# Twelve late rounds of a fused attention-and-experts kernel: scores in two halves, U as three fp32r passes, softmax by pairs of tiles, silus in another place

## The chip, the cores and the metric

The kernel runs on one core of a Trainium2 chip. The metric is device time in microseconds (us) of one execution; lower is better. Times are given as the median of the runs shown. TensorE (PE) has a clock that the chip grants at one of two levels, 1.2 or 2.4 GHz; the profile shows the granted one as a share of full speed.

## The reference, cut to what matters

Eight sequences of 1024 tokens with 256 features. Each token is normalised; then attention runs over the four heads of one token (not over tokens), and the rows are laid out anew afterwards; a mixture of eight experts with top-2 gates gives the factor of its output.

```python
xn = layernorm(x)
q = (xn @ Wq + bq).reshape(b, s, h, d)           # h = 4, d = 256; k and v in the same way
qr, qi, kr, ki = q * cos, q * sin, k * cos, k * sin
scores = (einsum('bshd,bsgd->bshg', qr, kr) + einsum('bshd,bsgd->bshg', qi, ki)) / sqrt(d)
out = einsum('bshg,bsgd->bshd', softmax(scores), v)
out = swapaxes(out, 1, 2).reshape(b, s, h * d) @ Wo + bo
y = xn + sum over the top 2 experts e of gate_e * (relu(xn @ wg[e]) * (xn @ wp[e])) @ wo[e]
result = x + out * silu(y)
```

## The kernel before, in words

**Tiling.** The 8192 tokens are worked through in 16 rounds (q = 0 to 15, NQ = 16) of 512 tokens, four tiles of 128 each (n = 4q to 4q+3). Rounds 0 to 3 (QE = 4) run first, then the experts (135 tiles of 128 gathered tokens, each with its `up`, `ht` and `down`), then the twelve late rounds 4 to 15. Semaphores order everything; each engine follows its own written-out list, and nothing is moved by a scheduler.

**One late round on TensorE** (`segment` of the tensor block). Chunks c = 0 to 15 are projections: `L1082`, six fp32r matmuls of 512 columns each (two halves of the features times the three products of high and low parts, WH and WL of the weights, XH and XL of the tokens). Even-numbered and odd-numbered chunks hold the two halves of a head's features; c below 8 is q, the rest is k. ScalarE (`L819`, times cosine) and then VectorE (`L1598`, times sine) write the chunk rotated into QT. Chunks 16 to 23 are U, the tokens times M = Wv Wo folded per head, 512 columns each: `L1093`, two fp32 matmuls whose operands are XTJ (the sum of XH and XL in another order, made by GpSimd at `L578`) and M_s in SBUF. ScalarE copies each U chunk to UN (`L826`), SyncE writes it to `u_d` (`L325`) and loads it back in another layout as US (`L399`). Between the U chunks stand the mixes of the round before (`mix`, `L1050`: attention weights AT times US) and the transposes `xt` of the round after. Then come `scores` of four tiles, 32 fp32 matmuls of 64 columns each (`L1029`), on which VectorE does `soft_a`, ScalarE the Exp (`L840`), VectorE `soft_b`; `spread` builds AT for a tile in the next round.

**PSUM.** There are eight banks. A projection or U chunk may take its bank when ScalarE and VectorE are through with the chunk that had it before (`ring`). Projections of the late rounds take five banks in turn.

**The output of a round.** GpSimd's list for iteration q is `xtj(q)`, `total(q - 1)` (16 multiplies and adds of 128x256 on expert outputs that were loaded: `L663`, `L667`, `L670`), in rounds 5, 7, 9, 11 (`host`) also `total` of one of the early rounds, and `finish(q - 1)` (`L678`, `L679`). `total(q - 1)` feeds a Silu on ScalarE (`L806`; `silu(q - 1)`), placed after chunk 18 of round q, and that feeds `finish`. The Silu of an early round (`L802`) stands among the Exps behind the scores of a host round. SyncE's list at the end of round q, behind the last write of U, is: three loads of US, `reload_e` (`L443`, waits for the early Silu) or `store_e` (`L451`) in rounds 5 to 12, `store_c(q - 1)` (`L410`, waits for `finish(q - 1)`), `load_c(q)`: expert outputs and tokens (`L422` to `L424`) and, once the store has landed (same buffers), the x rows (`L428`). `total(q)` waits for all of `load_c(q)`.

In round 15 the mixes of its own tiles follow at the end, with a last `store_last`.

## Time and profile before

| | us |
|---|---|
| median of 3 runs | 1589.56 (1588.63 to 1591.09) |
| the profiled execution | 1596.37 |
| its span, first to last instruction | 1594.6 |
| late rounds: first projection of round 4 to the end of the span | 1009.4 to 1594.6 |

The profiled execution has 1.8 us around its span and lies 6.8 us above the median. TensorE is busy 96% of the span, VectorE 61%, GpSimd 50%, ScalarE 46%. In the rows, a fp32 matmul shows as two records, a matmul's duration overlaps the next one's, so that pace is read from starts; SPq rows are issues of DMAs by SyncE. Times in the timelines count from the start of the span.

### The profile page before, as it was taken

To read this page: it belongs to the slowest core of one execution; us is meant where nothing else is said; L and a number is where in the kernel's file an instruction comes from. 1 tells how busy PE (TensorE), PEld (TensorE's weight loads), DVE (VectorE), ACT (ScalarE), POOL (GpSimd) and SP (SyncE) were. 2 spreads that over 40 slices of the span, in tenths; PEclk is the share of its full clock that TensorE was granted. 3 is DMA by queue.
4 is the path that set the end of the run, shared out by engine and by line. 5 is a ranking of instruction groups with operands and counts; after the bars stand their busy time and mean duration, and the time that the engine had idled before them with its cause. 6 is when DMAs were issued, how large, how long until landed. Compare 5 with 4: busy or idle time off the path is not lost.

```text
span 1594.6 us, 32793 instructions
## 1 busy us (share of the span) xinstructions
PE 1533.0 (96%) x11408; PEld 1168.2 (73%) x11408; DVE 976.4 (61%) x1880; ACT 729.6 (46%) x1205; POOL 794.2 (50%) x945
## 2 busy tenths in 40 slices
PE   5999699989999999999999999999999999999997
PEld 2546565658888888888888888776666776666774
DVE  7567899953333333333333333577889788888777
ACT  4766334413333333333333333546456565555552
POOL 4637588913344434443344333253584564853456
PEclk9999899989999999999999999999999999999998
DMA  9989842266133232223211231255555666455464
GB/s 326 395 316 331 299 175 72 75 206 209 56 132 96 96 113 76 88 102 112 78 54 57 71 145 44 91 165 176 179 181 180 201 197 226 149 164 168 148 205 146
DMA packets 175351, 251.23 MB, mean 158 GB/s; under 512 B 15336, under 2 KB 122656, under 8 KB 175072
## 3 DMA queue, kind: packets, MB, share of 16 engines
q1 hardware_dynamic: 160576, 211.48, 38.8%
q0 software_dynamic: 12960, 35.41, 6.7%
q8 instruction: 104, 1.70, 0.4%
q10 hardware_dynamic: 1664, 2.26, 0.4%
q14 instruction: 47, 0.39, 0.1%
HBM read 149.58 MB, written 99.50 MB: 156 GB/s over the span
## 4 chain that ended last, share of the span: by engine, by line
PE 90%; DVE 6%; DMA 1%; ACT 1%; issue 1%; SPq 1%; ACTq 0%; DVEq 0%
PE ps L1147 24%; PE ps L1082 21%; PE ps L1093 13%; PE ps L1166 12%; PE ps L1029 7%; PE ps L1156 4%; PE ps L1050 2%; PE ps L1129 2%; PE ps L998 2%; PE ps L926 1%; PE ps L982 1%; PE ps L916 1%; DVE UN L1232 1%; DMA WR<-w_d 1%; DVE OH L1555 1%
## 5 line engine op out<-in xcount | busy, mean ns | idle before, releaser
L1147 PE MATMUL ps<-WR,FR 128*128 x1620 | 407.6, 401 | 2.3 <-DMA WR<-w_d 2.3
L1147 PEld LDWEIGHTS ps<-WR,FR 128*128 128x128 f32 x1620 | 295.8, 189 | 59.9 <-issue 2.5
L651 POOL DMA_INDIRECT y_d<-AUX x135 | 133.3, 987 | 353.0 <-ACT AUX L870 353.0
L1658 DVE TENSOR_TENSOR AUX<-AUX,ps 128x512 f32<-128x512 f32 x135 | 93.0, 689 | 341.2 <-ACT AUX L858 341.2
L819 ACT ACTIVATE WM<-ps,bcs,trig 128x512 f32<-128x512 f32 x256 | 253.1, 1016 | 90.7 <-PE ps L1082 83.4
L1598 DVE TENSOR_SCALAR WM<-ps,vec,trig 128x512 f32<-128x512 f32 x256 | 244.4, 993 | 62.7 <-ACT WM L819 62.0
L1093 PE MATMUL ps<-WM,XTJ 128*128 128x512 f32 x512 | 237.1, 600 | 0.0
L858 ACT ACTIVATE AUX<-ps 128x512 f32<-128x512 f32 x135 | 80.9, 599 | 317.5 <-PE ps L1147 282.8
L1082 PE MATMUL ps<-XH,WH 128*128 128x512 f32 x512 | 205.2, 401 | 4.8 <-issue 3.8
L1166 PE MATMUL ps<-WR,ABR 128*128 x1080 | 209.4, 292 | 0.0
L1082 PE MATMUL ps<-XL,WH 128*128 128x512 f32 x512 | 200.2, 391 | 0.0
L1082 PE MATMUL ps<-XH,WL 128*128 128x512 f32 x512 | 200.0, 391 | 0.0
L646 POOL DMA_INDIRECT AUX<-xn_d,AUX x135 | 131.6, 975 | 75.3 <-issue 40.0
L1166 PEld LDWEIGHTS ps<-WR,ABR 128*128 128x128 f32 x1080 | 165.5, 190 | 0.0
L1093 PEld LDWEIGHTS ps<-WM,XTJ 128*128 128x128 f32 x512 | 91.6, 190 | 96.6 <-issue 93.8
L663 POOL TENSOR_TENSOR AUX<-AUX,GP 128x256 f32<-128x256 f32 x128 | 81.2, 669 | 150.1 <-DMA AUX<-in_L_attn_x_dram 145.4
L1166 PE MATMUL ps<-WR,FR 128*128 x540 | 152.0, 281 | 0.0
L1029 PE MATMUL ps<-WM 128*64 128x64 f32 x4096 | 131.4, 228 | 18.0 <-DVE TM L1486 16.7
L1029 PEld LDWEIGHTS ps<-WM 128*64 128x64 f32 x4096 | 127.4, 143 | 26.9 <-DVE TM L1486 17.1
L826 ACT ACTIVATE UN<-ps 128x512 f32<-128x512 f32 x128 | 76.2, 595 | 139.4 <-PE ps L1093 135.9
L1082 PEld LDWEIGHTS ps<-XH,WH 128*128 128x128 f32 x512 | 96.6, 189 | 25.7 <-issue 5.0
L1082 PEld LDWEIGHTS ps<-XH,WL 128*128 128x128 f32 x512 | 96.5, 189 | 20.6
(238 smaller groups left out, 2202.9 us busy)
## 6 DMA issues: line engine op xcount, KB each, us to landing
US<-u_d SPq DMA_DIRECT2D x63, 512.0 KB, 4.8
u_d<-UN SPq DMA_DIRECT2D x120, 256.0 KB, 2.0
WR<-w_d SPq DMA_DIRECT2D x96, 256.0 KB
AUX<-y_d SPq DMA_DIRECT2D x32, 512.0 KB, 5.5
WM<-in_L_attn_x_dram SPq DMA_DIRECT2D x16, 512.0 KB, 9.6
xn_d<-WM SPq DMA_DIRECT2D x32, 256.0 KB, 7.4
w_d<-USR SPq DMA_DIRECT2D x16, 512.0 KB, 4.2
AUX<-xn_d SPq DMA_DIRECT2D x16, 512.0 KB, 6.1
```

Source lines behind the costliest of these rows:

```text
L646: e.indirect_dma_start(XG[m % 4], None, xn_d, bass.IndirectOffsetOnAxis(gidx[:, m:m + 1], 0)).then_inc(s_g[m % 4], 16)
L651: e.indirect_dma_start(y_d, bass.IndirectOffsetOnAxis(toks[:, n:n + 1], 0), YS[n % 4], None).then_inc(s_y[n % 4], 16)
L663: ins = e.tensor_tensor(y[:, i, :], y[:, i, :], GP[:, i, k, q, None].broadcast_to([128, D]), ALU.mult)
L819: e.activation(rotated(2 * x, i), b, ACT.Identity, bias=bcs[:, x, 0, i:i + 1], scale=trig[:, 0, i:i + 1]).then_inc(s_ca, 1)
L858: e.activation(GR[:, :], mG[m % 2][:, :], ACT.Relu).then_inc(s_gr, 1)
L1029: mm = e.matmul(pS[n % 2][row:row + 64, 64 * c:64 * c + 64].rearrange("p (g t) -> p g t", g=H), QT[:, x, h, col:col + 64], QT[:, 2 + x, h, ...
L1082: mm = e.matmul(b[:, :], w[:, k, 128 * c:128 * c + 128], xx[:, k, :], start=(k == 0 and w is WH and xx is XH), stop=(k == 1 and w is WL))
L1093: mm = e.matmul(b[:, :], XTJ[:, k, a // 2, :], M_s[:, k, 512 * a:512 * a + 512], start=(k == 0), stop=(k == 1))
L1147: mm = e.matmul(b[:, :], x, WR[:, bass.ds(off[m] + (2048 * z + 1024 * a + 512 * k), 512)], start=(k == 0 and x is xh and z == 0), stop=(k ...
L1166: mm = e.matmul(mY[m % 2][:, 0:256], x, WR[:, bass.ds(off[m] + (4096 + 1024 * z + 256 * c), 256)], start=(c == 0 and x is hh and z == 0), ...
L1598: e.tensor_scalar(rotated(2 * x + 1, i), ps[bank(24 * q + c)][:, :], bqk[:, x, i:i + 1], trig[:, 1, i:i + 1], ALU.add, ALU.mult).then_inc( ...
L1658: e.tensor_tensor(HS[:, m % 2, :], GR[:, :], mP[m % 2][:, :], ALU.mult).then_inc(s_h, 1)
```

## The change

Only the late rounds (q from 4 on) and the expert stage are changed.

- **U in three fp32r passes.** In the expert stage ScalarE's queue loads M from `m_d` in 16 pieces, VectorE splits each into a high and a low part (`split_m`), ScalarE's queue stores both in `mhl_d`. Behind the experts' weights SyncE loads the low part to ML and the high part to MH (in place of M_s). A U chunk is then six fp32r matmuls: XHJ by MH, XHJ by ML, XLJ by MH, for both halves of the features. GpSimd's `xj` makes XHJ and XLJ with eight copies of 256 columns (before: `xtj`, four additions).
- **Order of a round.** Rounds 4 to 14: the eight even chunks, U 16 to 19, first half of all scores (`half_scores(q, 0)`, step 24), the eight odd chunks, U 20 to 23, second half. Round 15: even chunks, all of U, first half, odd chunks, second half, then its mixes. QT becomes QH, half the size, which the odd chunks fill again. The number of score matmuls is the same; all four tiles gather in two banks.
- **Banks.** Even chunks take 0,1,6,7,2,0,1,2 (round 4: 0,1,4,5,2,0,1,2), odd ones 1,2,6,7,0,1,2,0.
- **Mixes** stand behind chunk 19, step 24, chunk 21 and chunk 23 (before: 18, 20, 22, 23); transposes behind 20 and 22 (before: 17, 20).
- **VectorE** does `soft_a2`, `soft_b2`, `spread2` for two tiles in one instruction each; one Exp serves two tiles.
- **Silus on ScalarE.** `silu(q - 1)` stands at step 24: behind the copy of U 19 and ahead of the eight odd rotations. `silu(host[q])` stands behind U 20. In round 15, `silu(15)` stands behind chunk 5 of the odd ones, and the x rows of round 15 are loaded late (`load_x`).

The diff, cut to its core:

```diff
+        def order(q):
+            if q < QE:
+                return tuple(range(24))
+            if q < NQ - 1:
+                return P0 + (16, 17, 18, 19) + P1 + (20, 21, 22, 23)
+            return P0 + tuple(range(16, 24)) + P1
+        BANKS = {c: (0, 1, 6, 7, 2, 0, 1, 2)[i] for i, c in enumerate(P0)}
+        BANKS.update({c: (1, 2, 6, 7, 0, 1, 2, 0)[i] for i, c in enumerate(P1)})
...
+            def xj(q):
+                e.wait_ge(s_xtd, 2 * q + 2)
+                e.wait_ge(s_ch, 24 * q)
+                for k in range(2):
+                    for v, w in ((XHJ, XH), (XLJ, XL)):
+                        for j in range(2):
+                            ins = e.tensor_copy(v[:, k, 2 * j:2 * j + 2, :],
+                                                w[:, k, :].rearrange("p (r j) -> p j r", j=4)[:, 2 * j:2 * j + 2, :])
+                    ins.then_inc(s_xtj, 1)
...
-                    for c in range(24):
-                        e.wait_ge(s_ch, 24 * q + c + 1)
-                        b = ps[bank(24 * q + c)][:, :]
+                    for c in steps(q):
+                        if c == 24:
+                            if q > QE:
+                                silu(q - 1)
+                            continue
+                        e.wait_ge(s_ch, at(q, c))
...
-                        if q > QE and c == 18:
-                            silu(q - 1)
-                        if q == NQ - 1 and c == 23:
+                        if q == NQ - 1 and c == 5:
                             silu(q)
+                        if q in host and c == 20:
+                            silu(host[q])
...
+            def split_m(i):
+                e.wait_ge(s_mr, 16 * (i + 1))
+                ch(e.tensor_copy(UNR[:, 1, :], UN[:, 0, :]))
+                e.tensor_tensor(UNR[:, 2, :], UN[:, 0, :], UNR[:, 1, :].bitcast(F32), ALU.subtract).then_inc(s_msp, 1)
...
                             for k in range(2):
-                                mm = e.matmul(b[:, :], XTJ[:, k, a // 2, :], M_s[:, k, 512 * a:512 * a + 512],
-                                              start=(k == 0), stop=(k == 1))
+                                for xx, w in ((XHJ, MH), (XHJ, ML), (XLJ, MH)):
+                                    mm = e.matmul(b[:, :], xx[:, k, j, :], w[:, k, cols],
+                                                  start=(k == 0 and xx is XHJ and w is MH), stop=(k == 1 and xx is XLJ))
```

ScalarE's list for one late round of the kernel before, from the end of one round's projections on (L819 rotation, L826 copy of U, L755 copy of the transposed tokens, L806 Silu of the round before with its table load, L840 Exp):

```order
L819 ACTIVATE WM<-ps,bcs,trig 128x512 x16
L826 ACTIVATE UN<-ps 128x512 x2
L755 ACTIVATE XH<-ps 128x512
L826 ACTIVATE UN<-ps 128x512
L806 ACT_TABLE_LOAD
L806 ACTIVATE AUX<-AUX 128x1024
L826 ACTIVATE UN<-ps 128x512 x2
L755 ACTIVATE XH<-ps 128x512
L826 ACTIVATE UN<-ps 128x512 x3
```

The same stretch of the changed kernel (L926 rotation, L935 copy of U, L855 tokens, L906 Silu, L949 Exp):

```order
L926 ACTIVATE WM<-ps,bcs,trig 128x512 x8
L935 ACTIVATE UN<-ps 128x512 x4
L906 ACT_TABLE_LOAD
L906 ACTIVATE AUX<-AUX 128x1024
L926 ACTIVATE WM<-ps,bcs,trig 128x512 x8
L935 ACTIVATE UN<-ps 128x512
L855 ACTIVATE XH<-ps 128x512
L935 ACTIVATE UN<-ps 128x512 x2
L855 ACTIVATE XH<-ps 128x512
L935 ACTIVATE UN<-ps 128x512
```

The Silu stood behind all sixteen rotations and three copies of U; now eight rotations stand behind it.

ScalarE's last round of the changed kernel, where both Silus of the end stand:

```order
L926 ACTIVATE WM<-ps,bcs,trig 128x512 x8
L935 ACTIVATE UN<-ps 128x512 x8
L906 ACT_TABLE_LOAD
L906 ACTIVATE AUX<-AUX 128x1024
L926 ACTIVATE WM<-ps,bcs,trig 128x512 x3
L906 ACTIVATE AUX<-AUX 128x1024
L926 ACTIVATE WM<-ps,bcs,trig 128x512 x5
L949 ACT_TABLE_LOAD
L949 ACTIVATE AC<-AC 128x32 x2
```

In the kernel before, the last Silu stood behind the last copy of U, with no rotation after it; now five rotations and the second half of the scores follow.

TensorE's list at the end of a late round, before (L1093 U, L1050 mix, L1029 scores, all four tiles):

```order
L1093 MATMUL ps<-WM,XTJ 128x512 x4
L1050 MATMUL ps<-US,AT 32x256 x4
L1093 MATMUL ps<-WM,XTJ 128x512 x2
L1050 MATMUL ps<-US,AT 32x256 x4
L1029 MATMUL ps<-WM 64x64 x128
```

And in the changed kernel (L1260 U, L1114 transposes, L1204 mix, L1181 half of the scores):

```order
L1114 MATMUL ps<-ident,XB 128x128 x4
L1260 MATMUL ps<-WR,XHJ 128x512 x2
L1260 MATMUL ps<-WR,ABR 128x512
L1260 MATMUL ps<-WR,XHJ 128x512 x2
L1260 MATMUL ps<-WR,ABR 128x512
L1204 MATMUL ps<-US,AT 32x256 x4
L1181 MATMUL ps<-WM 64x64 x64
```

One U chunk is six matmuls where it was two, and 64 instead of 128 score matmuls lie between the last write of U and the next round's first projection.

## Rows read from the trace of the kernel before

**Rows 1.** TensorE's timeline (start, duration, engine, line, operation): projections.
```profile
1009.40 0.47 PE L1082 MATMUL ps<-XH,WH 128*128 128x512 f32 x1
...
1056.42 0.50 PE L1082 MATMUL ps<-XH,WH 128*128 128x512 f32 x1
...
1246.32 0.50 PE L1082 MATMUL ps<-XH,WH 128*128 128x512 f32 x1
...
1251.67 0.39 PE L1082 MATMUL ps<-XH,WL 128*128 128x512 f32 x1
1251.90 0.39 PE L1082 MATMUL ps<-XH,WH 128*128 128x512 f32 x1
```

**Rows 2.** TensorE's timeline: scores of round 4; first U and last mix of round 8.
```profile
1048.81 7.68 PE L1029 MATMUL ps<-WM 128*64 128x64 f32 x256
...
1220.18 3.59 PE L1093 MATMUL ps<-WM,XTJ 128*128 128x512 f32 x8
...
1237.18 0.64 PE L1050 MATMUL ps<-US,AT 128*32 128x256 f32 x8
```

**Rows 3.** ScalarE's timeline: rotations; Silu and last U copy of round 8.
```profile
1106.68 10.13 ACT L819 ACTIVATE WM<-ps,bcs,trig 128x512 f32<-128x512 f32 x9
...
1219.02 0.78 ACT L819 ACTIVATE WM<-ps,bcs,trig 128x512 f32<-128x512 f32 x1 [0.58 <-PE ps L1082]
...
1226.58 1.28 ACT L806 ACT_TABLE_LOAD   x1
1227.87 1.06 ACT L806 ACTIVATE AUX<-AUX 128x1024 f32<-128x1024 f32 x1
...
1237.29 0.60 ACT L826 ACTIVATE UN<-ps 128x512 f32<-128x512 f32 x1 [1.89 <-PE ps L1093]
```

**Rows 4.** SyncE's timeline: issues at the end of rounds 5, 8, 14.
```profile
1088.93 7.40 SPq L325 DMA_DIRECT2D u_d<-UN  x4
...
1237.91 0.32 SPq L325 DMA_DIRECT2D u_d<-UN  x1
...
1241.59 4.13 SPq L451 DMA_DIRECT2D out_dram<-AUX  x4
1245.76 3.56 SPq L410 DMA_DIRECT2D out_dram<-AUX  x4
...
1251.32 2.73 SPq L428 DMA_DIRECT2D AUX<-in_L_attn_x_dram  x4
...
1516.15 7.39 SPq L325 DMA_DIRECT2D u_d<-UN  x4
```

**Rows 5.** GpSimd's timeline: totals of rounds 7 and 8, tokens for U.
```profile
1214.10 5.38 POOL L663 TENSOR_TENSOR AUX<-AUX,GP 128x256 f32<-128x256 f32 x8 [16.07 <-DMA AUX<-in_L_attn_x_dram]
...
1222.42 3.82 POOL L670 TENSOR_TENSOR AUX<-AUX 128x256 f32<-128x256 f32 x4
...
1239.89 4.53 POOL L578 TENSOR_TENSOR XTJ<-XH,XL 128x256 f32<-128x256 f32 x4
1259.32 4.61 POOL L663 TENSOR_TENSOR AUX<-AUX,GP 128x256 f32<-128x256 f32 x8 [14.90 <-DMA AUX<-in_L_attn_x_dram]
...
1266.91 2.80 POOL L670 TENSOR_TENSOR AUX<-AUX 128x256 f32<-128x256 f32 x4
```

**Rows 6.** VectorE's timeline: a strided and a plain rotation.
```profile
1208.07 1.19 DVE L1598 TENSOR_SCALAR WM<-ps,vec,trig 128x512 f32<-128x512 f32 x1 [0.19 <-ACT WM L819]
...
1219.83 0.81 DVE L1598 TENSOR_SCALAR WM<-ps,vec,trig 128x512 f32<-128x512 f32 x1 [0.55 <-ACT WM L819]
```

**Rows 7.** TensorE's timeline in round 15: first projection, two mixes.
```profile
1530.68 0.50 PE L1082 MATMUL ps<-XH,WH 128*128 128x512 f32 x1
...
1578.10 0.66 PE L1050 MATMUL ps<-US,AT 128*32 128x256 f32 x8 [2.81 <-DVE AT L1513]
...
1586.48 1.10 PE L1050 MATMUL ps<-US,AT 128*32 128x256 f32 x8 [2.71 <-DVE AUX L1540]
```

**Rows 8.** One window of 1 us (granted clock third from the end).
```profile
1580.00:1581.00 1.00, 1.00 (x25) 1.00 (x24) 0.90 (x4) 0.00 (x0) 0.19 (x1) 0.50 0.99 340
```

More of the change, by code:

```diff
@@ L428, in load_c, with load_x @@
                     e.dma_start(xx[h:128:4], rows(xf, q)[h]).then_inc(sl, 16)
+            def load_x():
+                e.wait_ge(s_ch, at(NQ - 1, 17))
+                for h in range(H):
+                    e.dma_start(cs(NQ - 1)[3][h:128:4], rows(xf, NQ - 1)[h]).then_inc(s_xe, 16)
             def load_e(k):
@@ L840, in segment @@
                         e.activation(SE[:, n % 2, :], SS[:, n % 2, :], ACT.Exp, scale=1.0 / 16).then_inc(s_exp, 1)
-                        if i == 1 and q in host:
-                            silu(host[q])
             e.wait_ge(s_trig, 1)
@@ L1033, in scores, with half_scores @@
                 mm.then_inc(s_s, 1)
+            def half_scores(q, h):
+                e.wait_ge(s_ca, at(q, 14 + h))
+                e.wait_ge(s_cd, rotated_by[q, 14 + h])
+                if h == 0:
+                    e.wait_ge(s_sm1, 4 * q)
+                for i in range(4):
+                    for c in range(4):
+                        for x in range(2):
+                            for a in range(2):
+                                row = 64 * a
+                                col = 128 * (4 * i + c) + row
+                                to = 256 * (i % 2) + 64 * c
+                                mm = e.matmul(pS[i // 2][row:row + 64, to:to + 64].rearrange("p (g t) -> p g t", g=H),
+                                              QH[:, x, col:col + 64],
+                                              QH[:, 2 + x, :].rearrange("p (g t) -> p g t", g=H)[:, :, col // 4:col // 4 + 16],
+                                              start=(h == x == c == i % 2 == 0),
+                                              stop=(h == x == i % 2 == 1 and c == 3))
+                    if h == 1:
+                        mm.then_inc(s_s, 1)
             def mix(n):
@@ L1076, in segment @@
                     e.wait_ge(s_xtd, 2 * q + 2)
-                    for c in range(24):
-                        b = ring(24 * q + c)
+                    for c in steps(q):
+                        if c == 24:
+                            half_scores(q, 0)
+                            if c in mixes(q):
+                                mix(4 * q - 4 + mixes(q)[c])
+                            continue
+                        b = ring(q, c)
                         if c < 16:
@@ L1109, in segment @@
                         scores(4 * q + i)
[L1110 to L1111 removed]
                         place(lists.get((q, 24 + i), ()))
                 if q1 == NQ:
[L1114 to L1115 removed]
+                    e.wait_ge(s_ca, at(NQ - 1, 15))
+                    e.wait_ge(s_cd, rotated_by[NQ - 1, 15])
+                    for i in range(4):
+                        mix(4 * NQ - 4 + i)
             e.wait_ge(s_wsp, 4)
@@ L1613, in segment @@
                             early(host[q - 1])
-                        if q + 1 < q1 and c in (17, 20):
-                            xt(q + 1, c // 20)
+                        if q + 1 < q1 and c in turns(q):
+                            xt(q + 1, turns(q)[c])
+                    n = 4 * q
+                    if q >= QE:
+                        soft_a2(n)
+                        soft_a2(n + 2)
+                        soft_b2(n)
+                        if q < NQ - 1:
+                            soft_b2(n + 2)
+                            continue
+                        spread2(n)
+                        soft_b2(n + 2)
+                        spread2(n + 2)
+                        for i in range(4):
+                            mixed(n + i)
+                        continue
                     if q == QE - 1:
@@ L1629, in segment @@
                     soft_b(4 * q + 3)
-                if q1 == NQ:
-                    spread(4 * NQ - 1)
-                    for i in range(1, 4):
-                        mixed(4 * NQ - 4 + i)
             segment(0, QE)
```

247 lines of the change are left out of this document (192 added, 55 removed).

## The prediction

> **What bounds the kernel now.** I read the page first: TensorE is busy 96% of the span and the chain that ended last is 90% TensorE. Then TensorE's timeline, round by round. An undisturbed late round lasts 1056.42 - 1009.40 = 47.0 us from first projection to first projection [rows 1], and no gap of note is in it, so TensorE bounds the late rounds. A cut of its work is therefore worth its full size, until something else sets the round. To find what that is I followed, in the timelines of ScalarE, SyncE and GpSimd, the one loop that runs from round to round beside TensorE: last U copy, SyncE's queue, load, `total`, Silu. In the kernel before it has hardly any slack: the total of round 7 ends at 1222.42 + 3.82 = 1226.24, and the Silu that waits for it starts at 1227.87, behind a table load from 1226.58 on [rows 3, 5]. The reader should see there that the data come late, and that only the place of the Silu, 27 us into the round, hides it. The change moves this place.
>
> **TensorE's saving.** U: eight records of a fp32 matmul take from 1220.18 on 3.59 us, of which 0.16 overlaps what follows, so 0.43 each [rows 2]; 32 records per round make 13.7 us. The three passes are 8 x 6 = 48 fp32r matmuls of 512 columns. Their nearest row is the projection, same size and type: 1251.90 - 1251.67 = 0.23 [rows 1], exactly 1.36 per chunk of six, so 10.9 us. Saved: 2.8 us, and with one mix and two transposes breaking up U no more often than before I take 3.0, a round of 44.0 us. Scores keep their 128 matmuls, 7.7 us [rows 2], 3.85 per half; mixes (0.57 each, 1237.75 - 1237.18) and transposes are moved only. Bounds for a U chunk: 1.36 and the 1.72 of now, since nothing else of that kind is in the trace; I take the first. Twelve rounds would gain 36 us if nothing else decided.
>
> **Expert stage.** Added there: 16 loads and 16 stores on ScalarE's queue, 32 VectorE instructions (about 1 us per seven tiles), 12.6 MB of transfers and 4 MB more of loads. From 560 to 1030 us TensorE is busy without a break while VectorE is busy under 40%, ScalarE likewise, and the DMA engines a quarter. A tile takes 4.8 us and each product of VectorE is wanted most of a tile later. Cost zero; were that cover gone it would be 16 us at most. The M parts are in SBUF long before round 4, as the experts' last 17 tiles lie behind the last expert load.
>
> **xj.** Eight GpSimd copies replace four strided additions of 4.53 us together, 1.1 each [rows 5]. A copy reads one operand: between 0.4 and 1.1 us each, 3 to 9 us. It starts with the last mixes of a round, some 4 us ahead of the next one's start, and U now wants it 10.9 us into the round instead of 21.8. It fits even at 9 us. Zero.
>
> **Where the stall goes: the Silu.** `silu(q-1)` now stands behind U 19 [the order of ScalarE], that is 10.9 (even chunks) + 5.4 (four U) + 1 = 17.5 us into the round; before, 27. Behind it are the eight odd rotations. While ScalarE waits there, TensorE goes on with the first half of the scores, a mix and the five odd chunks whose banks are free (1, 2, 6, 7, 0), and then stands still at chunk 11, which wants bank 1 from chunk 1. I work out the loop from the last U write of one round to that of the next, as if it closed:
>
> 1. Last U write to total done. Round 8: the write is issued by 1238.23, then come the loads of US, `store_e`, `store_c`, the loads of `load_c` (last x issue ends at 1254.05), landing, total from 1259.32 to 1269.71 [rows 4, 5]: 31.5 us. The same reading in rounds 6, 10, 12, 13, 14 gives 29.7, 30.5, 29.4, 29.3, 30.2. In host rounds SyncE also waits 4 to 6 us for the early Silu; without this wait, which the change removes, and with an unslowed total they give 28.4 to 30.1. Mean of all ten: 29.7.
> 2. A total that runs beside VectorE's `spread` and `biased` is slower: 1214.10 to 1226.24 is 12.1 us against 10.4 for 1259.32 to 1269.71 [rows 5]. In the changed order it runs 16 to 27 us into the round, beside three `biased` and one `spread2`. Between 0 and 1.7; I take 1.4.
> 3. Silu: 1.06, table load already done while waiting, hop 0.1 [rows 3]: 1.2.
> 4. From the Silu's end to the next last U write. ScalarE's strided rotations take 1.17 each (10.13 less one of 0.78, over 8) [rows 3], VectorE follows 0.19 later with 1.18 [rows 6]. So chunk 1 leaves bank 1 at 2.6 and TensorE does chunk 11 until 4.0 and 13 until 5.4; chunk 15 wants bank 0 from chunk 9, free at 6.9 (four strided rotations and a plain one, VectorE's at 0.81), and ends at 8.3. Then four U (5.4), two transposes (0.9), one mix (0.6): 15.3; copy and issue 1.0 as at 1237.29 to 1238.23 [rows 3, 4]: 16.3.
>
> Sum 29.7 + 1.4 + 1.2 + 16.3 = **48.6 us per round**, above the 44.0 of TensorE's own work: the loop does close, and TensorE loses 4.6 us in each round. In the kernel before, the nine rounds from the last U write of round 5 (1096.33) to that of round 14 (1523.54) [rows 4] took 427.2, or 47.5 each.
>
> **The clock.** TensorE stands still for about 3 us at chunk 11. After a gap of 2.81 us the trace shows the granted clock at 0.50, that is 1.2 GHz, in a window that begins 2 us behind the gap [rows 7, 8]. If that happens here, chunks 11 and 13 take about 1.7 us more, but chunk 15 waits for VectorE until 6.9 anyway, so 0.2 is left. Zero in the sum.
>
> **The total.** Round 4 has no Silu and gains 3.0. Round 5's total is ready early (loaded long before), so its end of U comes 2.2 earlier: TensorE's saving twice, 6.0, less the half of the scores that now stands ahead of the last U. Rounds 6 to 14: 9 x 48.6 = 437.4, against 427.2: +10.2. Round 15, from the last U write of round 14: before 1594.6 - 1523.5 = 71.1. After: 3.3 to the round's start (half a set of scores), then 27.9 for even chunks, U, half the scores and four mixes; odd chunks run, but `silu(15)` behind chunk 5 wants a second total, which GpSimd ends at 27.8 + 10.4 = 38.2; Silu until 39.4, chunks 7 and 9 rotated until 42.6, chunk 15 until 44.1, rotated by 46.0, second half of the scores until 49.9. Then softmax and spread of pairs, about 4.8 (VectorE's pieces of two tiles), four mixes at the low clock, 1.96 each (1586.48 to the next at 1588.4 by its records) [rows 7], and 3.5 for the last product and store: 66, and 1 for scores at the low clock after the long wait. 70.3, so -0.8. Sum: -2.2 + 10.2 - 0.8 = **+7.2 us**. The profiled span would be 1601.8; the median, 6.8 below the profiled execution before, goes from 1589.56 to **1596.8 us**. What 0.1 us in the loop means here: 0.9 us in the end.
>
> **A rule of the skill.** The rows show a total slowed by 1.7 us by about four us of VectorE work in SBUF. The Trainium skill (SBUF — State Buffer, "SBUF: two separate sides") says that a VectorE instruction with two SBUF inputs and a GpSimd one that reads SBUF exclude each other for the whole instruction. By it, an estimate, the three `biased` (1.2 each) and two products would hold the total up by their full 4 us instead of 1.4; that result is the fourth rival below.
>
> **Rivals.**
> 1. *The saving arrives* (not slower): something makes the total come in time, and the round is TensorE's 44.0. What decides is whether loop parts 1 to 3 end within 28 us of the last write. Eleven rounds at -3.0, the last one as above without its 5 us stall: about -35, 1555 us. Against it: the shortest of ten readings is 28.4, before any slowing and the Silu. Chance 0.09.
> 2. *A shorter loop*: parts 1 and 2 at their low ends (28.6 and 0), the last part 0.5 less because VectorE's rotations overlap by 0.1 each: 46.2 to 47.4. 9 x -1.2 to -2.4 off the forecast: 1575 to 1586 us. For it: SyncE no longer waits for the early Silus, so transfers may spread better. Chance 0.17.
> 3. *The low clock counts*: it falls at chunk 11 and again at chunk 15, and the four U of the last part run at 1.2 GHz too: 1.7 us more in each of nine rounds, +15: 1612 us. For it: a gap of 2.8 us has been enough in the trace. Against it: chunks 11 to 15 are nearly unbroken work. Chance 0.10.
> 4. *GpSimd and VectorE exclude each other*: a total held up by 4 us instead of 1.4: 9 x 2.6 = 23, but in the rows both slow a little, and the 12.1 us total had as much beside it. 1620 us. Chance 0.04.
> 5. *The change does not do what it says*: U's passes cost as much as fp32, or xj comes late. Behind the stall both have some cover of their own, so the time stays near 1600. Chance 0.02, counted with the forecast.
>
> **How the numbers follow.** The forecast (loop closes at 47.5 to 49.9) has 0.60; of it 0.45 are slower by over 0.2%, 0.13 within, 0.02 faster. A difference of 0.2%, 3.2 us, is about what a measurement of this kernel can tell from none. Rivals 3 and 4 are slower (0.14), rival 1 faster (0.09), rival 2 faster with 0.15 and within with 0.02. Together: faster 0.26, same 0.15, slower 0.59. The range: loop bounds 47.5 to 49.9 give 1587 to 1609; rival 2 and rival 3 up to 1614 are taken in, so 1574 to 1614; rival 1, rival 4 and the tails are left out, about 0.18.
>
> **What the profile after would show.** Right: ScalarE idle ahead of the first odd rotation for 8 to 10 us in rounds 6 to 14, put down to GpSimd's last addition or to the Silu; TensorE's projections of odd chunks waiting for VectorE's rotation, two gaps of 2 to 3 and 1 to 2 us per round; first projections 48 to 49 us apart, but 44 from round 4 to round 5; U passes 0.23 apart; DMA landing 15 us into a round. Wrong: rounds of 44 us, a total that starts before 10 us into the round, or a gap that ends with GpSimd's xj ahead of U 16.

## The result, and the profile after

| | before | after |
|---|---|---|
| median, us | 1590.12 (4 runs beside it) | **1625.3** (4 runs, 1618.91 to 1630.5) |
| ratio to before | | **1.0205**, 95% interval 1.0178 to 1.0232 |
| span of the profiled execution, us | 1594.6 | 1628.7 |
| mean granted clock | 0.986 | 0.979 |
| round 4, first projection to first projection, us | 47.0 | 44.3 |
| rounds 5 to 14, the same, mean, us | 47.4 | 50.7 |
| round 15, first projection to the end, us | 63.9 | 68.8 |

The kernel became 2% slower. The forecast had the sign and the place right and was 28 us short: 1596.8 us forecast, and the time lies above the range of 1574 to 1614. Of the 35 us that the change costs it had seen 7.

TensorE's timeline of the kernel after (start, duration, engine, line, operation), at the first projection of rounds 4, 5 and 6. These rows answer to [rows 1]:

```profile
1008.47 0.47 PE L1241 MATMUL ps<-XH,WH 128*128 128x512 f32 x1
...
1052.74 0.50 PE L1241 MATMUL ps<-XH,WH 128*128 128x512 f32 x1
...
1104.79 0.50 PE L1241 MATMUL ps<-XH,WH 128*128 128x512 f32 x1
```

The reader sees the promised saving once: 1052.74 - 1008.47 = 44.3 us for round 4, against 47.0. The next one takes 52.1. One round in detail, number 8. TensorE (answers to [rows 2]):

```profile
1223.00 0.39 PE L1260 MATMUL ps<-WR,ABR 128*128 128x512 f32 x1
...
1223.68 0.39 PE L1260 MATMUL ps<-WR,ABR 128*128 128x512 f32 x1
...
1224.57 3.95 PE L1181 MATMUL ps<-WM 128*64 128x64 f32 x128
...
1235.75 0.39 PE L1241 MATMUL ps<-XH,WL 128*128 128x512 f32 x1
1239.14 0.59 PE L1241 MATMUL ps<-XH,WH 128*128 128x512 f32 x1 [3.00 <-DVE WM L1810]
1239.53 0.63 PE L1241 MATMUL ps<-XL,WH 128*128 128x512 f32 x1
```

Three U passes take 1223.68 - 1223.00 = 0.68, so 0.23 each, and a half of the scores 3.95: both as forecast. Then TensorE stands still for 3.00 us ahead of chunk 11, and goes on at 0.39 to 0.43 a matmul, from start to start, where it was 0.23. ScalarE in the same round (answers to [rows 3]); the number in brackets is the idle time ahead of an instruction, and what ended it:

```profile
1225.21 0.60 ACT L935 ACTIVATE UN<-ps 128x512 f32<-128x512 f32 x1 [1.87 <-DMA u_d<-UN]
1225.83 1.28 ACT L906 ACT_TABLE_LOAD   x1
1235.56 1.06 ACT L906 ACTIVATE AUX<-AUX 128x1024 f32<-128x1024 f32 x1 [8.45 <-POOL AUX L769]
```

GpSimd's total, which the Silu waits for (answers to [rows 5]):

```profile
1223.16 5.26 POOL L762 TENSOR_TENSOR AUX<-AUX,GP 128x256 f32<-128x256 f32 x8 [14.43 <-DMA AUX<-in_L_attn_x_dram]
1228.51 3.00 POOL L766 TENSOR_TENSOR AUX<-AUX 128x256 f32<-128x256 f32 x4
1231.59 3.94 POOL L769 TENSOR_TENSOR AUX<-AUX 128x256 f32<-128x256 f32 x4
```

And SyncE's U writes that close the loop, the last of round 7 and of round 8 (answers to [rows 4]):

```profile
1199.06 3.30 SPq L395 DMA_DIRECT2D u_d<-UN  x3
...
1247.13 6.13 SPq L395 DMA_DIRECT2D u_d<-UN  x4
```

The loop can be read off: last write ends at 1202.36, total from 1223.16 to 1235.53, Silu from 1235.56 to 1236.62, next last write ends at 1253.26. That is 20.8 + 12.4 + 1.1 + 16.6 = 50.9 us. The waits in sum, TensorE's and ScalarE's from 1009 to 1629 us (engine, line, what was waited for: us, times, longest):

```profile
PE ps L1241 <- DVE WM L1810: 32.2, 21, 3.5
...
ACT AUX L906 <- POOL AUX L769: 67.1, 11, 9.4
...
ACT UN L935 <- DMA u_d<-UN: 26.0, 6, 8.2
```

### The profile page after: what moved, and what is told of

Read it like the earlier page. It is cut to its first block, busy times and chain, and to the rows that moved or that the text cites. A ratio compares the mean times of both kernels' runs of the same rounds, so it can differ in the third digit from the quotient of the medians.

```text
span 1628.7 us, 33088 instructions
## 1 busy us (share of the span) xinstructions
PE 1519.5 (93%) x11600; PEld 1211.5 (74%) x11600; DVE 933.3 (57%) x1640; ACT 702.6 (43%) x1173; POOL 813.7 (50%) x993
## 4 chain that ended last, share of the span: by engine, by line
PE 65%; POOL 9%; DMA 8%; DVE 7%; SPq 6%; ACT 3%; issue 2%; ACTq 0%; DVEq 0%; POOLq 0%
PE ps L1318 23%; PE ps L1337 12%; PE ps L1241 10%; POOL AUX L762 4%; PE ps L1260 4%; PE ps L1327 4%; POOL AUX L769 3%; DMA out_dram<-AUX 3%; DMA AUX<-in_L_attn_x_dram 3%; POOL AUX L766 2%; PE ps L1256 2%; PE ps L1300 2%; PE ps L1130 2%; DVE WM L1810 2%; PE ps L1058 1%
## 5 line engine op out<-in xcount | busy, mean ns | idle before, releaser
L750 POOL DMA_INDIRECT y_d<-AUX x135 | 138.9, 1029 | 347.1 <-ACT AUX L983 347.1
L1810 DVE TENSOR_SCALAR WM<-ps,vec,trig 128x512 f32<-128x512 f32 x256 | 233.9, 993 | 83.6 <-ACT WM L926 83.3
L926 ACT ACTIVATE WM<-ps,bcs,trig 128x512 f32<-128x512 f32 x256 | 237.9, 1011 | 92.2 <-PE ps L1241 89.4
L1241 PE MATMUL ps<-XH,WH 128*128 128x512 f32 x512 | 213.3, 417 | 40.0 <-DVE WM L1810 33.1
L1241 PE MATMUL ps<-XL,WH 128*128 128x512 f32 x512 | 205.2, 401 | 0.0
L762 POOL TENSOR_TENSOR AUX<-AUX,GP 128x256 f32<-128x256 f32 x128 | 90.4, 740 | 136.2 <-DMA AUX<-in_L_attn_x_dram 133.0
L935 ACT ACTIVATE UN<-ps 128x512 f32<-128x512 f32 x128 | 76.5, 598 | 145.3 <-PE ps L1260 79.8
L1260 PE MATMUL ps<-WR,XHJ 128*128 128x512 f32 x384 | 123.7, 403 | 7.8 <-issue 4.9
L1241 PEld LDWEIGHTS ps<-XL,WH 128*128 128x128 f32 x512 | 99.4, 194 | 18.3 <-issue 0.2
L691 POOL TENSOR_SCALAR OH<-AUX 128x128 bf16<-128x128 f32 x96 | 95.1, 1002 | 23.9 <-DVE AUX L1604 15.6
L1181 PEld LDWEIGHTS ps<-WM 128*64 128x64 f32 x3072 | 93.6, 140 | 16.3 <-issue 12.9
```

The costliest lines, as they stand in the source:

```text
L691: e.tensor_scalar(rank1h[:, j % 16, :], ior_f, slot_p[:, k, n:n + 1], mark[:, k, n:n + 1], ALU.is_equal, ALU.mult).then_inc(s_oa, 1)
L750: e.indirect_dma_start(y_d, bass.IndirectOffsetOnAxis(toks[:, n:n + 1], 0), YS[n % 4], None).then_inc(s_y[n % 4], 16)
L762: ins = e.tensor_tensor(y[:, i, :], y[:, i, :], GP[:, i, k, q, None].broadcast_to([128, D]), ALU.mult)
L926: e.activation(rotated(q, 2 * x, i), b, ACT.Identity, bias=bcs[:, x, 0, i:i + 1], scale=trig[:, 0, i:i + 1]).then_inc(s_ca, 1)
L1181: mm = e.matmul(pS[i // 2][row:row + 64, to:to + 64].rearrange("p (g t) -> p g t", g=H), QH[:, x, col:col + 64], QH[:, 2 + x, :].rearrange ...
L1241: mm = e.matmul(b[:, :], w[:, k, 128 * c:128 * c + 128], xx[:, k, :], start=(k == 0 and w is WH and xx is XH), stop=(k == 1 and w is WL))
```

## The experiments

All experiment kernels share one small edit of the expert stage (how two engines read a count). The first run shows that it costs nothing, and the others are read against it. "A round" in the table is the mean of rounds 5 to 14, from first projection to first projection.

| kernel | median, us | ratio to before (95%) | a round, us |
|---|---|---|---|
| control: after, with this edit | 1624.13 | 1.0218 (1.0192 to 1.0245) | 50.1 |
| Silus later | 1595.83 | 1.0028 (1.0008 to 1.0048) | 46.8 |
| total without its products | 1591.68 | 1.0007 (0.9988 to 1.0026) | 46.5 |
| loads for the total first | 1609.05 | 1.0123 (1.0085 to 1.0161) | 48.9 |
| before, with an early Silu | 1675.83 | 1.0547 (1.0525 to 1.0569) | 55.6 |
| total of quarter 4 behind the softmax | 1618.69 | 1.0186 (1.017 to 1.0203) | 49.5 |
| no bias added beside the total | 1596.56 | 1.0036 (1.002 to 1.0052) | 48.0 |
| early quarter's loads later, alone | 1628.1 | 1.0235 (1.0217 to 1.0252) | 50.4 |
| Silus later and three repairs | 1575.43 | 0.9913 (0.9897 to 0.993) | 45.9 |
| the same, early quarter's loads later | **1567.6** | **0.9863** (0.9844 to 0.9883) | 45.3 |
| the same, loads for the total first | 1576.76 | 0.993 (0.991 to 0.9949) | 45.7 |

### Control

```diff
-                e.reg_load(wreg[m % 2], ewl[0:1, m:m + 1])
-                e.wait_ge(s_wl, e.snap(wreg[m % 2], min_val=192, max_val=192 * E))
+                e.wait_ge(s_wl, e.value_load(ewl[0:1, m:m + 1], min_val=192, max_val=192 * E))
```

> The changed kernel with only the two register reads of the expert stage written in another form (TensorE's count of expert loads, SyncE's count of tiles): nothing of the late rounds is touched. Every theory expects 1625 us within 4, the same 50.6 us per late round and the same expert stage. It is the base from which the other runs are read.

Measured 1624.13 us. The late rounds show the same waits: ScalarE 61.8 us for GpSimd's last addition, nine times.

### Undo the place of the Silu

```diff
                         if c == 24:
-                            if q > QE:
+                            if q == NQ - 1:
                                 silu(q - 1)
...
-                        if q in host and c == 20:
+                        if QE < q < NQ - 1 and c == 20:
+                            silu(q - 1)
+                        if q in host and c == 23:
                             silu(host[q])
```

> Only the place of the Silu on ScalarE changes, in rounds 5 to 14: silu(q-1) from behind U 19 to behind U 20's copy (after the odd rotations), the Silu of an early round's quarter from behind U 20 to behind U 23. Theory (the loop last U write, load, total, Silu, rotations, last U write sets the round only because eight rotations stand behind the Silu): total is done 33 us after the last write, that is about 30 us into the round, and U 20 is copied at about 37, so nothing waits; rounds fall from 50.6 to 44.0 to 45.0, nine of them by 50 to 59 us, time 1566 to 1578 us. Rival 1 (the halves of the scores, the softmax by pairs and the banks cost the 6.6 us per round): under 5 us of change. Rival 2 (the later Silu makes finish, the store and the next load later, and the loop closes again at about 47): 1590 to 1600 us.

Measured 1595.83: 28 us less than the control, not 50. The mechanism is confirmed and the size missed. ScalarE no longer waits for a total in rounds 5 to 14: each Silu of rounds 6 to 14 starts 8 to 11 us behind the end of its total. ScalarE's list of waits from 1053 to 1560 us has:

```profile
ACT WM L923 <- PE ps L1240: 79.7, 72, 6.3
...
ACT UN L932 <- DMA u_d<-UN: 43.9, 11, 9.4
```

The list has no line for the Silu any more. TensorE's own list from 1053 to 1525 us shows what remains, single gaps of 1.1 to 3.2 us and one small one per round (only behind the one of 1.91 us did the clock fall):

```profile
PE ps L1259 <- ACT WM L923: 5.2, 4, 1.6
PE ps L1180 <- issue: 4.5, 2, 2.6
PE ps L1240 <- DVE WM L1807: 3.9, 2, 3.2
```

Rival 2 names the time (1590 to 1600) but not the cause: the loop has slack here, since the Silu waits for nothing. What lies between 44.3 and 46.8 us per round is taken up below, with the repairs.

### Shorten the loop without touching the Silu

```diff
+                if q < QE:
                     for i in range(4):
                         for k, y in enumerate((y1, y2)):
                             ins = e.tensor_tensor(y[:, i, :], y[:, i, :], GP[:, i, k, q, None]...
```

> GpSimd's eight multiplications with the gates are left out of the total of quarters 4 to 15 (that part of the computation is missing); the Silu keeps its place. Theory (the loop decides): each loop is shorter by the 4.6 to 5.3 us of these eight, so rounds of 45.3 to 46.3 and 9 x 4.6 to 5.3 = 41 to 48 us less; round 5, where VectorE's subtraction of 5.19 us lies beside just these multiplications, gains another 4 to 5: 1572 to 1580 us. Rival (the total is not what decides): within 10 us of the control.

Measured 1591.68: 32 us less than the control, where 44 to 52 were expected (1572 to 1580 us). ScalarE's wait for the total falls from 61.8 to 16.8 us. Two edits that have nothing in common but the loop each take some 30 us away, so the loop set the round. The late Silus, with slack in the loop, show a second floor at 46.8 us, 2.5 above TensorE's 44.3. The 46.5 here is near it, but is not the same thing: in six of nine rounds the Silu still starts 0.03 us behind the total's end, and this profile is of the fastest execution (1580.7 us, 11 below the median).

### Shorten the loop on SyncE

```diff
-                        store_c(q - 1)
                         load_c(q)
...
                 e.dma_start(xn, blk(xn_d, q)).then_inc(sl, 16)
...
+                    store_c(q - 1)
                     e.wait_ge(s_o, 64 * (q - QE))
                 for h in range(H):
-                    e.dma_start(xx[h:128:4], rows(xf, q)[h]).then_inc(sl, 16)
+                    e.dma_start(xx[h:128:4], rows(xf, q)[h]).then_inc(s_cx, 16)
...
-                    e.wait_ge(*((s_cl, 112 * (q - QE + 1)) if q < NQ - 1 else (s_c15, 48)))
+                    e.wait_ge(*((s_cl, 48 * (q - QE + 1)) if q < NQ - 1 else (s_c15, 48)))
```

> SyncE issues the three loads that the total reads ahead of the four stores of the quarter before, and the total waits for these three alone, no longer for the four loads of x as well (which the later sum waits for). The Silu keeps its place. Theory (the loop decides, and its first part is SyncE's queue): the loads are issued 2.6 to 5.3 us earlier and the x loads (3 us) are no longer waited for, so the total starts 5 to 8 us earlier, 12 to 15 us behind the last write; rounds fall to 44 to 46, time 1570 to 1590 us. Rival (the loads are late for the transfers' own sake, or the total comes beside more VectorE work and gets slower): under 15 us of gain.

Measured 1609.05: 15 us less, on the edge of the rival. The total starts 14 to 18 us behind the last write, 3.3 earlier on average than in the control. In rounds 6, 8, 10, 12, 13 and 14 that shortens the loop, by 1.7 to 4 us. In rounds 7, 9 and 11, with an early quarter, it gets 1.4 to 2.8 us longer, as another wait takes the place of the old one. ScalarE and SyncE there:

```profile
1276.71 0.60 ACT L935 ACTIVATE UN<-ps 128x512 f32<-128x512 f32 x1 [12.81 <-DMA u_d<-UN]
...
1278.62 1.06 ACT L906 ACTIVATE AUX<-AUX 128x1024 f32<-128x1024 f32 x1
```

```profile
1262.93 2.62 SPq L503 DMA_DIRECT2D AUX<-in_L_attn_x_dram  x4
...
1268.72 0.51 SPq L517 DMA_DIRECT2D AUX<-xn_d  x1
```

The first U write stands on SyncE's queue behind the x loads, which wait for the stores, and behind the early quarter's loads. ScalarE waits 12.81 us for its U buffer and comes to the Silu 3.1 us after the total is done. I had counted what the edit takes off the loop, not what it puts ahead of the U writes.

### Only the place, in the kernel before

```diff
-                        if q > QE and c == 18:
+                        if q > QE and c == 9:
                             silu(q - 1)
```

> The kernel before, with one edit: in the late rounds silu(q-1) stands on ScalarE behind chunk 9 (14 us into the round) and no longer behind U 18 (27 us in). Nothing of the scores, of U or of the softmax is touched. Theory (the place of the Silu closes the loop whatever the forms are): total is done 30 us behind the last write, Silu 1.1, then rotations of chunks 10 to 15 and eight U of 1.8 and the write, about 20: a round of 50 to 52 against 47.4, so 25 to 40 us more, 1615 to 1630 us, with ScalarE waiting 8 to 12 us for GpSimd in each round. Rival (the new forms cost the time, the place alone does little): under 8 us more.

Measured 1675.83: 87 us more than the kernel before (1589.1 beside it), the direction of the theory and more than twice its size (25 to 40). ScalarE at a Silu, and SyncE at the last writes of two rounds:

```profile
1241.31 1.06 ACT L803 ACTIVATE AUX<-AUX 128x1024 f32<-128x1024 f32 x1 [11.52 <-POOL AUX L667]
```

```profile
1257.52 7.39 SPq L325 DMA_DIRECT2D u_d<-UN  x4
...
1311.62 7.40 SPq L325 DMA_DIRECT2D u_d<-UN  x4
```

The last writes end at 1206.63, 1264.91 and 1319.02. The second step, 54.1 us, is 29.9 (write to total done) + 1.1 + 23.1 (Silu to next last write): I had put the last part at 20. The first, 58.3, has 34.6 in its first part, because in these rounds SyncE also waits for the early quarter's Silu, which stood late in the kernel before. So the same formula gives these rounds too. It also shows what the change did beside moving the Silu: behind it stand 16 us in the kernel after, against 23 here, with four U chunks already done.

### Round 5: GpSimd keeps VectorE out

```diff
+                if q == QE + 1:
+                    e.wait_ge(s_sa2, 4 * QE + 4)
                 if QE < q < NQ:
                     total(q - 1)
```

> The changed kernel with one wait more: in round 5 GpSimd begins the total of quarter 4 only when VectorE has ended the softmax of round 4. Theory (a GpSimd multiplication in a row keeps VectorE's short subtraction out for 5 us, and this holds up the first rotation of round 5): the subtraction takes 0.3 to 0.7 us, the first rotation starts 5 us earlier, TensorE's gap of 3.17 us at 7.5 us into round 5 goes, with 1 to 2 us of low clock, and the time falls by 4 to 6 us: 1618 to 1621. Rival (the subtraction is slow for another reason): no change, 1624.

Round 5 of the kernel after has a row that no one expected. VectorE, then GpSimd:

```profile
1052.51 0.19 DVE L1702 TENSOR_REDUCE AC<-AC 128x8 f32<-128x32 f32 x1
1052.80 5.19 DVE L1703 TENSOR_TENSOR AC<-AC 128x32 f32<-128x32 f32 x1
```

```profile
1053.32 4.63 POOL L762 TENSOR_TENSOR AUX<-AUX,GP 128x256 f32<-128x256 f32 x8
1058.02 2.81 POOL L766 TENSOR_TENSOR AUX<-AUX 128x256 f32<-128x256 f32 x4
```

A subtraction of 32 columns takes 5.19 us and ends with the last of GpSimd's eight multiplications. The second pair's softmax, both Exp and ScalarE's first rotation stand behind it, and TensorE waits 3.17 us at chunk 11. With the wait added the same subtraction reads:

```profile
1050.74 0.60 DVE L1700 TENSOR_TENSOR AC<-AC 128x32 f32<-128x32 f32 x1
```

TensorE's gap in round 5 is gone and the time is 5.4 us less than the control's, as expected. The edit moves the total away from the softmax and changes nothing else there.

### What the total costs beside VectorE

```diff
                 u = US[:, n % 3, :, :]
+                if n >= 16:
+                    u = US[:, n % 3, 0:1, 0:8]
+                    e.tensor_tensor(u, u, BR[:, None, 0:8], ALU.add).then_inc(s_ub, 1)
+                    return
```

> The changed kernel with its Silu where it stands; VectorE's addition of the bias row to U (128x1024, 1.2 to 2.5 us, once per tile) is cut to eight columns from quarter 4's tiles on, so most of the bias is missing there. Theory (beside VectorE's additions the total is slowed from 10.4 to 13.1 us, and each us of it is a us of the loop): total 10.4 to 11.4 us, rounds shorter by 1.7 to 2.7, nine of them 15 to 24: 1600 to 1609 us. Rival (the slower total is not VectorE's doing, or the loop has slack there): totals stay at 13 and the time within 4 us of 1624.

Measured 1596.56: 27.6 us less than the control, more than the 15 to 24 expected. GpSimd's total in round 8 of this kernel:

```profile
1214.79 4.61 POOL L759 TENSOR_TENSOR AUX<-AUX,GP 128x256 f32<-128x256 f32 x8 [16.32 <-DMA AUX<-in_L_attn_x_dram]
1219.49 2.78 POOL L763 TENSOR_TENSOR AUX<-AUX 128x256 f32<-128x256 f32 x4
1222.34 3.05 POOL L766 TENSOR_TENSOR AUX<-AUX 128x256 f32<-128x256 f32 x4
```

10.6 us. The nine totals of rounds 6 to 14 take 10.6 to 11.0 in this kernel, where those of the kernel after take 11.8 to 13.9. The nine rounds 6 to 14 shrink from 50.2 in the control to 47.9 each, 21 us: 2.1 of the 2.4 per round is the shorter total (12.9 to 10.7), and 0.4 lies behind the Silu, where the clock stays at full speed in all nine rounds of this kernel. Another 4.5 us is in round 15, where a total of 14.3 us comes down to 10.7. VectorE's part that was left out is 1.2 us of work per tile and is hardly ever late itself (TensorE waits 0.7 us for it in the whole kernel after): it costs time through GpSimd.

### The early quarter's loads, and the repairs

> The changed kernel, only with the three loads of the early quarter behind the fourth U write in rounds 5, 7, 9 and 11; every Silu keeps its early place. Theory (the loop through the Silu decides, what is gained ahead of it is waited out at it): ScalarE's wait for the U buffers goes, its wait for the total grows by as much, TensorE's gaps put down to issue shrink; 0 to 6 us less, 1618 to 1624. Rival (SyncE's queue in these four rounds was the cost, as the last run suggests with its 8 us): 8 to 12 us less, 1612 to 1616.

```diff
-                    if q in host:
-                        load_e(host[q])
...
                         write_u(e, q, c)
+                        if q in host and c == 3:
+                            load_e(host[q])
```

Measured 1628.1, 4 us more than the control. ScalarE's waits from 1053 to 1560 us:

```profile
ACT AUX L903 <- POOL AUX L766: 77.3, 9, 9.3
ACT UN L932 <- DMA u_d<-UN: 12.7, 7, 2.8
```

In the control these are 61.8 and 31.7. What ScalarE no longer waits for its buffers it waits for the total: the loop takes back all that is gained ahead of it. TensorE's gaps within the scores shrink too, from 1.67 and 2.58 us in rounds 9 and 11 of the control to 0.30 and nothing above 0.3, and the time does not. The rival (8 to 12 us less) falls. The theory's mechanism holds, its number does not: 0 to 6 us less were expected, and why it is 4 more is open.

The repairs on top of the later Silus, beside the wait of round 5 shown above:

```diff
-                        if q - 1 in host and c == 8:
+                        if q - 1 in host and c == 22:
                             early(host[q - 1])
...
-                        if q == NQ - 1 and c == 5:
+                        if q == NQ - 1 and c == 15:
                             silu(q)
```

> The later Silus of the run above (1595.8 us), with three more edits: the wait of round 5 as in the run beside it; the host quarter's two VectorE sums (2.4 us) from behind chunk 8 to behind U 22, out of the way of the even rotations; silu(15) from behind chunk 5 to behind chunk 15. Theory (what is left over TensorE's 44.3 per round are small stalls, each followed by a stretch at half clock): round 5 gains 4 to 5; rounds 6, 8, 10 and 12 lose their gap of 1.1 to 1.6 us ahead of U 16 and gain 1.5 to 2.5 each, 8 together; round 15 loses its gap of 3.9 us ahead of chunk 7 and gains 3 to 4: 1578 to 1581 us, 12 faster than the kernel before. Rival (another stall takes their place, or the loop closes again): 1590 or more.

Measured 1575.43, a little better than expected. TensorE's gaps of 1.1 to 1.6 us ahead of U 16 in rounds 6, 8, 10 and 12 are gone, and so are those of 3.2 us in round 5 and 3.9 us in round 15. The three edits were made together; what each is worth was not measured here, only the wait of round 5 by itself above. With the early quarter's loads moved as well:

> As the run beside it, and in rounds 5, 7, 9 and 11 the three loads of the early quarter (1.5 MB) stand on SyncE behind the fourth U write and no longer ahead of the first. Theory (TensorE's gaps in the middle of the scores, 1.9 to 2.6 us and put down to issue, come from its instruction block being read beside a full DMA ring): less is in flight 20 us into these rounds, the gaps there shrink or go, 2 to 4 us each with the half clock behind them, 4 to 10 us together. Rival (the instruction reads are late whatever is in flight, or the ring is as full with the loads later): no change within 2 us.

Measured **1567.6 us, 1.4% faster than the kernel before** and 3.5% faster than the changed one. The same edit that was worth nothing alone is worth 7.8 us here. Rounds 9 and 11, 49.0 and 48.1 us without it, take 45.3 and 45.4. TensorE at the same place of round 11, without and with the later loads:

```profile
1343.95 3.25 PE L1182 MATMUL ps<-WM 128*64 128x64 f32 x104
1350.24 0.92 PE L1182 MATMUL ps<-WM 128*64 128x64 f32 x24 [3.04 <-issue]
```

```profile
1338.87 3.25 PE L1182 MATMUL ps<-WM 128*64 128x64 f32 x104
1342.41 0.92 PE L1182 MATMUL ps<-WM 128*64 128x64 f32 x24 [0.30 <-issue]
```

Finally the loads for the total first, on top of that:

> The fastest version so far (1567.6 us) with the loads for the total issued ahead of the stores as well. Theory (with the later Silus the loop has some 8 us of slack, so an earlier total buys nothing): within 3 us of 1567.6. Rival (U buffers now wait behind the x loads, as they did with this edit alone, and some of it reaches TensorE): 3 to 12 us slower, 1571 to 1580.

Measured 1576.76, 9 us slower: the rival. ScalarE waits 71.0 us for its U buffers (35.0 without the edit), and TensorE 4.26 us ahead of a U chunk in round 15. With slack in the loop an earlier total buys nothing, and its price stays.

## Why the prediction was wrong in size and right in kind

**TensorE's saving** (3.0 per round, a round of 44.0): right. 44.3 us for round 4, passes 0.23 apart, half scores 3.9. The expert stage and `xj` at zero: right; TensorE is busy for 440.00 us of the window 560 to 1000 in both kernels, and the eight copies take 4.8 us and are early.

**The stall at the Silu, and that the loop closes:** right. The later Silus and the total without products take 28 and 32 us away. ScalarE waits for the total in every round from 6 to 14: 7.9 to 9.4 us in six of them, where 8 to 10 were forecast, and 2.6 to 4.9 in rounds 7, 9 and 11, where it waits for a U buffer first. TensorE's gap at chunk 11 is 1.3 to 3.5 us (none in round 7); ahead of chunk 15 it is 0.7 us or none, where 1 to 2 were forecast.

**The sum of the loop** (48.6 forecast, 50.6 measured; it is worked here as the mean of the nine loops from the last write of round 5, 1101.39, to that of round 14, 1556.47):

| part | forecast | measured | times nine |
|---|---|---|---|
| last write to total's start | 19.3 | 19.95 | +5.8 |
| the total | 10.4 + 1.4 | 13.1 | +11.8 |
| Silu and hop | 1.2 | 1.1 | -0.9 |
| Silu's end to last write | 16.3 | 16.4 | +1.1 |

The step that failed is number 2, **the contention term of 1.4 us**: measured it is 2.7, which makes 11.8 of the 27 us missed. I took it from one total beside VectorE (12.1 us, with 4.0 us of VectorE instructions recorded beside it that have both inputs in SBUF) and made that one the upper bound as well. The trace of the kernel before had dearer rows. The other three late totals with VectorE beside them take 11.5, 12.4 and 12.5 us, and the four totals of early rounds that ran in full beside VectorE's spreads take 13.5 to 13.6, 3.1 over the 10.4 of a total with nothing beside it. One of these (GpSimd, first and last of three groups):

```profile
1173.06 5.69 POOL L663 TENSOR_TENSOR AUX<-AUX,GP 128x256 f32<-128x256 f32 x8
...
1182.72 3.82 POOL L670 TENSOR_TENSOR AUX<-AUX 128x256 f32<-128x256 f32 x4
```

In the kernel after, 3.4 to 6.8 us of such VectorE instructions are recorded beside the nine totals, 5.1 on average. The run without the bias confirms that the longer total is VectorE's doing and that each us of it is a us of the round. It was also the dearest term to get wrong, since it counts nine times and once more in round 15.

The last row of the table is right in part by luck. From the Silu's end to the last write it takes 16.0 us in rounds 10, 11 and 13, where the clock stays at full speed, and 16.5 to 16.7 in rounds 6, 8, 9, 12 and 14, where it falls behind the gap at chunk 11 (round 7: 16.6 at full clock). The forecast had 16.3 and the low clock at zero.

**Round 5** (last write 2.2 us earlier than before, at 1094.1): wrong, 1101.39, +7.3 us. The sum held TensorE's saving and had no term for VectorE's softmax meeting GpSimd's total, which starts here right behind `xj` because its data came long ago. In the kernel before, the same eight multiplications ran beside the softmax too, from 1052.92 on, and no subtraction there took more than 0.94 us; so nothing in that trace gave this price. Counted from the first projection of round 4, the last write of round 5 comes at 92.9 us in the kernel after, 89.9 in the control and 85.3 with the wait, against 84.7 forecast. So the meeting is worth 4.6 us. Of the 3.0 between the control and the kernel after, 1.7 are the clock: TensorE has the same gap of 3.17 us in both, only in the kernel after did the clock fall behind it, and chunks 11, 13 and 15 took it 6.8 us instead of 5.1. The rest is small gaps that only the kernel after has. The gap's end and a window behind it, first the kernel after, then the control (granted clock third from the end):

```profile
1063.04 0.77 PE L1241 MATMUL ps<-XH,WH 128*128 128x512 f32 x1 [3.17 <-DVE WM L1810]
...
1063.00:1068.00 5.00, 4.96 (x12) 3.94 (x13) 4.41 (x5) 3.06 (x4) 1.88 (x5) 0.50 0.49 158
```

```profile
1059.64 0.47 PE L1238 MATMUL ps<-XH,WH 128*128 128x512 f32 x1 [3.17 <-DVE WM L1805]
...
1059.60:1064.00 4.40, 3.69 (x15) 2.80 (x16) 4.40 (x6) 3.70 (x5) 2.60 (x6) 1.00 0.27 85
```

**Round 15** (70.3 from the last write of round 14): 72.2, +1.9, mostly for the same reason: total 14 takes 15.0 us beside VectorE, begins 1.7 us sooner behind the last write than worked out, and ends at 1589.11, 1.4 us later in the round.

Together 17.8 + 7.3 + 1.9 = 27 us, which is 1628.7 - 1601.8. The three stretches tile the span, so they must add up; they say where the time is, and the runs say why. The first part's 5.8 us (SyncE's issues and landings, 19.95 against 19.3) was taken apart by no run. The median is 28.5 us off, as it lies 5.2 us below this profiled execution and not 6.8.

Two sums of the prediction are off and decide nothing: the place of the Silu, 10.9 + 5.4 + 1, is 17.3 us and not 17.5, and rival 2's terms at their low ends give 45.6 us and not 46.2.

**The rivals.** Rival 1 (the saving arrives) and 2 (a shorter loop) did not happen. Rival 3, the low clock: the clock does fall, a window below shows 0.56, but in five of the nine rounds, and there it costs 0.6 us and not 1.7, since chunk 15 has to wait anyway. Rival 4 had a chance of 0.04 and named 1620 us: it was nearest, and its mechanism is at work. I had set it aside because in one row "both slow a little". With a total at 13.1 and a row of 5.19 us that reading does not hold. The Trainium skill (SBUF — State Buffer, "SBUF: two separate sides") says that a VectorE instruction with two SBUF inputs and a GpSimd one that reads SBUF exclude each other for the whole of the one that started first. The 5.19 us go further than this: the subtraction was kept out through eight multiplications in a row, until 1057.95. For the total no run here shows the rule in full size: it is longer by 2.7 us beside 5.1 us of such VectorE work, about half. VectorE's additions of the bias lengthen as well, from 1.22 us to 1.63 to 1.77 beside the total.

**What the sum did not see at all** is the second floor, 46.5 us, that rival 1 would have met: it would have given some 20 us less than it promised. The repairs took 1.5 us of it away (the host quarter's sums ahead of even rotations, the wait of round 5, the gaps within the scores). The last us, from 45.3 to 44.3, no run took apart.

## What to carry to other kernels

When a loop through several engines closes, cost each of its terms as carefully as the bound engine's own work: an error of 1 us in it is 1 us per round. Read a contention term from several rows, each with what stood beside it, and not from one. An edit that takes a wait away ahead of a closed loop is worth nothing by itself, and can be worth its full size once the loop is open: try it again then. Ahead of a queue, count what an edit puts in front of others, not only what it brings forward.

## What the runs showed of the hardware

**A row of GpSimd instructions can keep a VectorE instruction out to its end.** VectorE's subtraction of two SBUF tiles took 5.16 to 5.19 us beside eight multiplications in the six kernels that have this order, and 0.57 to 0.60 us apart from them. In the run without the products GpSimd does four additions there, and the subtraction ends with the last of these as well (VectorE, then GpSimd):

```profile
1050.21 3.40 DVE L1699 TENSOR_TENSOR AC<-AC 128x32 f32<-128x32 f32 x1
```

```profile
1050.71 2.86 POOL L764 TENSOR_TENSOR AUX<-AUX 128x256 f32<-128x256 f32 x4
```

Why the subtractions of the kernel before (16 columns each) slip in between the same multiplications, in 0.17 to 0.94 us, is open, and so is why the next subtraction of the same 32 columns takes 0.56 us beside the additions from 1058.02 on. The reverse direction: GpSimd's total takes 10.4 us with nothing beside it, 10.6 to 11.0 with little, and up to 15.0 (total 14) beside VectorE's additions.

**TensorE stands still longer within the scores when the DMA engines are full.** In the two rows of round 11 above, TensorE stops after the same 104th matmul, for 3.04 us or for 0.30. The DMA traffic around these rows, in stretches of 0.5 us (queue, packets, MB, share of 16 engines), from 1347.50 in the slow one:

```profile
q1 hardware_dynamic: 182, 0.18, 102.8%
q8 instruction: 1, 0.02, 12.0%
```

and from 1340.00 in the fast one:

```profile
q1 hardware_dynamic: 33, 0.06, 29.0%
q8 instruction: 1, 0.02, 12.1%
```

One instruction packet belongs to this place in both. With the engines full it comes 3.6 us or more after the burst of scores began at 1343.95, when TensorE has already stopped (1347.20); with the engines less busy it comes 1.1 to 1.6 us after the start at 1338.87. That TensorE waits for this packet, and the packet behind the data, is argued from these two cases and was not tried by itself. In the changed kernel too the gaps within the scores shrank when the loads were moved (the run above with that edit alone). The kernel before has such gaps as well, but the longest of its late rounds is 1.1 us; within the scores of the changed kernels they reach 3.1 us.

**The clock.** It fell behind some of TensorE's gaps and not behind others of the same length. It fell behind 3.00 us in round 8 of the kernel after, and behind 3.17 in round 5; it stayed at 1.00 behind 3.17 in round 5 of the control and behind 3.48 in round 11 of the kernel after. So a gap's length alone does not tell it here. In this window in round 8 the granted clock is the third number from the end. 0.56 as a mean says that most of it ran at 1.2 GHz instead of 2.4.

```profile
1239.00:1242.00 3.00, 2.86 (x7) 2.29 (x8) 3.00 (x4) 2.47 (x4) 0.74 (x1) 0.56 0.00 0
```

In the run with the later Silus a gap of 1.91 us within the scores, up to 1264.38, was enough:

```profile
1266.00:1268.00 2.00, 2.00 (x7) 1.51 (x6) 1.84 (x5) 0.65 (x2) 1.97 (x3) 0.50 0.41 144
```
